# W2's ternary blocks moved to the second turn and off GpSimd; odd relu pieces' upper halves written by ScalarE from PSUM

## The chip, the cores and the metric

The kernel runs on one core of one Trainium2 chip. The metric is the device time of one execution in microseconds (us), lower is better. TensorE, VectorE (DVE), ScalarE (ACT), GpSimd (POOL) and SyncE (SP) each run a queue of instructions of their own; they meet through semaphores. SyncE issues all DMAs.

## The reference

x has 8 sequences of 1024 rows of 512 values. A layer of attention with a compressive memory is followed by a feed-forward layer with ternary weights; each adds to x and ends in a layer norm.

```python
# attention, per segment of 128 rows, 8 heads of 64, carry (mem, z)
q, k, v = x @ Wq, x @ Wk, x @ Wv
sq, sk = elu(q) + 1, elu(k) + 1
att_mem = sq @ mem / (sq @ z)
mem, z = mem + sk.T @ v, z + sk.sum()
att = gate * att_mem + (1 - gate) * (softmax(q @ k.T / 8) @ v)
x = layernorm(x + att @ Wo)
# feed-forward: W -> clip(round(W / (mean|W| + eps)), -1, 1)
h = relu(x @ Wq1.T + b1)            # 2048 wide
x = layernorm(x + h @ Wq2.T + b2)
```

## The kernel before

**Turns.** A turn g (32 of them) takes two sequences' segments of 128 rows, in two halves t. Its steps are spread over three passes of one loop written for each engine, `for g in range(NG + 2)`: in pass g the attention of turn g runs (`project_qk`, `scores`, `project_v`, `turn_p`, `read_memory`, `attend`), the output projection of turn g-1 (`project_out`, then `residual` and `normalise` on VectorE), and the feed-forward of turn g-2 (`ffn_up`, `ffn_down`), whose first `ffn_up` pieces run at the end of pass g-1. The order of all calls in these loops is written out by hand, engine by engine. It, the semaphores and the four PSUM banks 2 to 5 that `take` deals out in rotation set the order of the work.

**fp32 by halves.** Each fp32 operand is an upper and a lower float16 part, and matmuls are done on both. `ffn_up(g, j)` (L430, L431) makes piece j of 8 of the hidden layer, 16 matmuls, in bank 0 or 1. `h_relu` (L1187) on ScalarE writes relu of it as fp32 into one of four buffers `h32`. `h_split` on VectorE converts it to float16 (`h_hi`, L858), and for even j subtracts (L861); for odd j `h_rest` on GpSimd subtracts (L1395). `ffn_down` (L444, L445) takes `h_hi` and `h_lo`.

**Ternary weights.** W1 and W2 are 16 blocks each. For each block two comparisons with a threshold are written as masks into the unused buffer `yt` (L912 below and L913 above on VectorE; for odd blocks the below mask on GpSimd, L1405). `turn_w` (L265, L266) turns and subtracts them in bank 0 or 1 by eight matmuls, and `put_w` (L1215) copies the result to `w1t` or `w2t`. The thresholds come from ScalarE's sums (`w_sum`, L1205) through `threshold` (L895) and `sum_all` (L486). Blocks 0 to 23 are compared in pass 0 and the last ones at its end and in pass 1.

**Copies on the DMA queue.** Transposes of whole tiles between 32x32 blocks are sixteen DMAs each: `move_y` (L1551, waits for both halves' norm), `move_sk` (L1563), `move_att` (L1551). Before and after `move_y` stand `bounce_out` and `bounce_back`: the next turn's maximum of x goes to DRAM and comes back to all partitions as `amax_row`. `update_memory` (L399) on TensorE waits for all sixteen sk copies; VectorE's `all_max` (L615), which stands ahead of `p_split` in its queue, waits for `amax_row`. The waiting lines read:

```python
pe.wait_ge(sem["skblocks"], MOVED * (g + 1))     # update_memory
sp.wait_ge(sem["norm0"], by_t(g, 1))             # move_y
pe.wait_ge(sem["relu"], n - 1)                   # ffn_up, n >= 2
```

## Time and profile before

| what | us |
|---|---|
| median of three runs | 1914.51 (1912.84 to 1919.87) |
| profiled execution, its own time | 1912.87 |
| its span | 1910.9 |
| TensorE busy | 1855.7 |
| VectorE busy | 1449.1 |
| ScalarE busy | 1006.1 |
| GpSimd busy | 794.7 |

The span is from the first to the last recorded instruction; the execution's own time has 2.0 us around it. Busy times add up an engine's instructions, in all stretches, so what a change is worth in one stretch is read from that stretch: from what ends the wait that comes last there.

### The profile page before, as it was taken

Reading aid. Unit: us, or ns where it says so; the run is one execution under the profiler, and the core shown is the slowest. Engines: PE = TensorE matmul, PEld = TensorE weight load, DVE = VectorE, ACT = ScalarE, POOL = GpSimd, SP = SyncE. Lnnn points to the kernel's source line nnn. Section 1 sums busy time; section 2 is a strip of 40 time slices with the busy share of each in tenths; the row PEclk is TensorE's granted clock in tenths of the full one; section 3 lists DMA queues with packets and bytes.
Section 4 is the critical chain, followed back from the end, with each engine's and each line's share of the span. In section 5 each row is a group of like instructions: output and inputs, shape, how many; then the busy total and the mean of one; then the engine's idle time right before and its main releaser. Section 6 shows DMA issues by size and latency. Waiting matters only on the chain.

```text
span 1910.9 us, 44707 instructions
## 1 busy us (share of the span) xinstructions
PE 1855.7 (97%) x16575; PEld 1311.8 (69%) x16575; DVE 1449.1 (76%) x2969; ACT 1006.1 (53%) x2426; POOL 794.7 (42%) x790
## 2 busy tenths in 40 slices
PE   5689999999999999999999999999999999999998
PEld 3566677766777766677766677766677766677765
DVE  7867777777777787777777877777777777777774
ACT  5755555555554555554555554545555645555541
POOL 1813344443344444344444344444345444344443
PEclk9889999999999999999999999999999999999999
DMA  8412333223333233233223333323333322333110
GB/s 270 123 23 46 58 61 66 52 49 59 62 59 65 49 53 61 58 60 65 54 45 64 61 59 64 64 38 60 61 59 63 67 38 59 61 58 62 36 23 23
DMA packets 556422, 117.49 MB, mean 61 GB/s; under 512 B 529824, under 2 KB 533808, under 8 KB 555696
## 3 DMA queue, kind: packets, MB, share of 16 engines
q1 hardware_dynamic: 556208, 114.64, 29.4%
q8 instruction: 134, 2.20, 0.6%
q14 instruction: 80, 0.66, 0.2%
HBM read 50.54 MB, written 16.80 MB: 35 GB/s over the span
## 4 chain that ended last, share of the span: by engine, by line
PE 80%; SPq 7%; DVE 6%; DMA 3%; issue 2%; ACT 1%; POOL 1%; DVEq 0%; POOLq 0%; ACTq 0%
PE bank L431 12%; PE bank L430 12%; PE bank L444 8%; PE bank L445 8%; SPq L1551 7%; PE bank L280 6%; PE bank L282 6%; PE bank L281 6%; PE bank L413 3%; PE bank L411 3%; PE bank L412 3%; PE bank L368 3%; DMA amax_row<-amax_dram 2%; PE bank L294 2%; PE bank L347 2%
## 5 line engine op out<-in xcount | busy, mean ns | idle before, releaser
L430 PE MATMUL bank<-yt,w1t 128*128 128x256 f16 x2048 | 453.9, 273 | 0.0
L431 PE MATMUL bank<-yt,w1t 128*128 128x256 f16 x2048 | 453.9, 273 | 0.0
L1141 ACT ACTIVATE prob<-bank,exp_bias,gscalars 128x128 f32<-128x128 f32 x512 | 227.6, 455 | 356.6 <-DVE exp_bias L723 347.7
L444 PE MATMUL bank<-w2t,arena 128*128 128x512 f16 x1024 | 388.4, 379 | 0.0
L445 PE MATMUL bank<-w2t,arena 128*128 128x512 f16 x1024 | 388.1, 379 | 0.0
L1187 ACT ACTIVATE arena<-bank,b_scaled,wscalars 128x256 f32<-128x256 f32 x512 | 262.9, 569 | 213.4 <-PE bank L431 156.3
L858 DVE CAST arena<-arena 128x512 f16<-128x512 f32 x256 | 154.8, 605 | 89.9 <-ACT arena L1187 89.1
L1317 POOL TENSOR_TENSOR att_mem<-att_mem,gate_in 128x512 f32<-128x512 f32 x60 | 83.1, 1385 | 330.1 <-DVE att_mem L762 318.7
L430 PEld LDWEIGHTS bank<-yt,w1t 128*128 128x128 f16 x2048 | 200.5, 98 | 23.3 <-issue 0.3
L431 PEld LDWEIGHTS bank<-yt,w1t 128*128 128x128 f16 x2048 | 200.3, 98 | 22.7
L1395 POOL TENSOR_TENSOR arena<-arena 128x512 f16<-128x512 f32 x128 | 155.3, 1213 | 87.6 <-DVE arena L858 87.6
L444 PEld LDWEIGHTS bank<-w2t,arena 128*128 128x128 f16 x1024 | 100.1, 98 | 111.9
L445 PEld LDWEIGHTS bank<-w2t,arena 128*128 128x128 f16 x1024 | 100.2, 98 | 110.5
L1353 POOL TENSOR_TENSOR at<-att_dot,at 128x512 f16<-128x512 f32 x60 | 89.7, 1495 | 191.3 <-ACT at L1160 191.3
L673 DVE SCALAR_TENSOR_TENSOR xt<-x_blocks,gscalars,xt 128x512 f16<-128x512 f32 x62 | 83.3, 1343 | 84.7 <-ACT xt L1095 84.7
L280 PE MATMUL bank<-xt,wk_hi 128*128 128x256 f16 x512 | 141.0, 275 | 0.0
L281 PE MATMUL bank<-xt,wk_hi 128*128 128x256 f16 x512 | 140.6, 275 | 0.0
L282 PE MATMUL bank<-xt,wk_lo 128*128 128x256 f16 x512 | 140.6, 275 | 0.0
L280 PE MATMUL bank<-xt,wq_hi 128*128 128x256 f16 x512 | 139.5, 273 | 0.0
L282 PE MATMUL bank<-xt,wq_lo 128*128 128x256 f16 x512 | 139.5, 273 | 0.0
L281 PE MATMUL bank<-xt,wq_hi 128*128 128x256 f16 x512 | 139.5, 273 | 0.0
L718 DVE TENSOR_REDUCE row_max<-bank 128x4 f32<-128x512 f32 x128 | 87.4, 683 | 37.6 <-PE bank L317 37.6
(191 smaller groups left out, 4392.9 us busy)
## 6 DMA issues: line engine op xcount, KB each, us to landing
rows<-in_L_attn_x SPq DMA_DIRECT2D x32, 512.0 KB, 3.6
out_rows<-rows SPq DMA_DIRECT2D x64, 256.0 KB, 2.3
x_blocks<-in_L_attn_x SPq DMA_DIRECT2D x248, 64.0 KB, 2.8
sk<-sk_t SPq DMA_DIRECT2D x480, 32.0 KB, 2.0
att_dot<-att_mem SPq DMA_DIRECT2D x480, 32.0 KB, 2.0
y_blocks<-rows SPq DMA_DIRECT2D x480, 32.0 KB
arena<-in_L_ffn_W SPq DMA_DIRECT2D x6, 1024.0 KB, 5.5
w2t<-in_L_ffn_W SPq DMA_DIRECT2D x2, 1024.0 KB, 13.3
```

The lines of the kernel that those rows point to most:

```text
L280: pe.matmul(ps[:, :, c], w_hi[n][:, k, cols], xt[:, :, k], start=k == 0, stop=False)
L281: pe.matmul(ps[:, :, c], w_hi[n][:, k, cols], xt[:, :, KT + k], start=False, stop=False)
L282: ins = pe.matmul(ps[:, :, c], w_lo[n][:, k, cols], xt[:, :, k], start=False, stop=k == KT - 1)
L430: pe.matmul(ps[:, c], w1t[:, k, cols], yt[:, g % 2, :, k], start=k == 0, stop=False)
L431: ins = pe.matmul(ps[:, c], w1t[:, k, cols], yt[:, g % 2, :, KT + k], start=False, stop=k == KT - 1)
L444: pe.matmul(banks[own][:], h_hi[:, f, toks], w2t[:, f, :], start=f == 0, stop=False)
L445: ins = pe.matmul(banks[own][:], h_lo[:, f, toks], w2t[:, f, :], start=False, stop=f == FT - 1)
L858: dve.tensor_copy(hi, h32[:, n % NH32]).then_inc(sem["h_hi"], 1)
L1141: ins = act.activation(prob[:, t, at], ps[:, c], ACT.Exp, scale=gcol(g, G_EXP), bias=exp_bias[:, t, at:at + 1], accum_out=row_sum[:, t, h: ...
L1187: ins = act.activation(h32[:, n % NH32, c * GT:(c + 1) * GT], ps[:, c], ACT.Relu, scale=w(H_SCALE_Y), bias=b1_scaled[:, f:f + 1])
L1395: pool.tensor_tensor(lo, h32[:, n % NH32], hi, ALU.subtract).then_inc(sem["h_pool"], 1)
L1551: sp.dma_start(to, at).then_inc(done, 16)
```

## The change

- No comparison is on GpSimd any more: VectorE does both of each block, with two pairs of masks instead of four. They lie in one half of `yt`, so that the first turn's `yt` can be written while W2's blocks are still made.
- W1's blocks (0 to 15) stay in pass 0. TensorE turns W2's (16 to 31) in pass 1 and, the last four, at the start of pass 2, in banks 6 and 7. `ffn_up` of turn 0 waits only for W1's blocks; `ffn_down` of turn 0 waits for all 32.
- For odd j, `h_relu` writes `h_hi` from PSUM by a second activation per half piece (L1196 there), and `h_split` is called for even j alone.
- The calls in all engines' loops stand in another order: `update_memory` now closes a pass, after `ffn_up` 0 to 2; on VectorE `normalise` of the first half stands before `group_max`; gates, two loads of W2 and two of x are issued a pass later.

```diff
-        wbelow = yt[:, 0].rearrange("p t k n -> p (t k n)").rearrange("p (b n) -> p b n", b=4)
-        wabove = yt[:, 1].rearrange("p t k n -> p (t k n)").rearrange("p (b n) -> p b n", b=4)
+        masks = yt[:, 1].rearrange("p t k n -> p (t k n)").rearrange("p (m b n) -> p m b n", m=2, b=2)
+        wbelow, wabove = masks[:, 0], masks[:, 1]
...
+        def turned_bank(n):
+
+            return banks[n % 2 if n < NBLOCKS // 2 else 6 + n % 2][:].rearrange("p (j c) -> p j c", j=4)
...
             def turn_w(n):
 
-                ps = banks[n % 2][:].rearrange("p (j c) -> p j c", j=4)
+                ps = turned_bank(n)
                 if n == 0:
                     pe.wait_ge(sem["ident16"], 1)
                 if n >= 2:
                     pe.wait_ge(sem["wput"], n - 1)
-                pe.wait_ge(sem["above"], n + 1)
-                pe.wait_ge(sem["below_pool" if n % 2 else "below"], n // 2 + 1)
+                if n == NBLOCKS // 2:
+                    pe.wait_ge(sem["hscale"], 1)
+                    pe.wait_ge(sem["thr_chain"], 2)
+                pe.wait_ge(sem["masks"], n + 1)
                 for j in range(4):
                     cols = slice(j * P, (j + 1) * P)
-                    pe.matmul(ps[:, j], wabove[:, n % 4, cols], ident16[:], start=True, stop=False)
-                    ins = pe.matmul(ps[:, j], wbelow[:, n % 4, cols], minus16[:], start=False, stop=True)
+                    pe.matmul(ps[:, j], wabove[:, n % 2, cols], ident16[:], start=True, stop=False)
+                    ins = pe.matmul(ps[:, j], wbelow[:, n % 2, cols], minus16[:], start=False, stop=True)
                 ins.then_inc(sem["wturn"], 1)
...
                 else:
-                    pe.wait_ge(sem["wput"], NBLOCKS)
+                    pe.wait_ge(sem["wput"], NBLOCKS // 2)
...
@@ -854,11 +860,12 @@
                 lo = h_lo[:, 2 * j:2 * j + 2].rearrange("p f t -> p (f t)")
                 if g and j == 0:
                     dve.wait_ge(sem["ffn2"], by_t(g - 1, 1))
+                if n == 0:
+                    dve.wait_ge(sem["masks"], NBLOCKS)
                 dve.wait_ge(sem["relu"], n + 1)
                 dve.tensor_copy(hi, h32[:, n % NH32]).then_inc(sem["h_hi"], 1)
-                if j % 2 == 0:
-                    dve.wait_ge(sem["h_hi"], n + 1)
-                    dve.tensor_tensor(lo, h32[:, n % NH32], hi, ALU.subtract).then_inc(sem["h_dve"], 1)
+                dve.wait_ge(sem["h_hi"], n // 2 + 1)
+                dve.tensor_tensor(lo, h32[:, n % NH32], hi, ALU.subtract).then_inc(sem["h_dve"], 1)
...
-                if n >= 4:
-                    dve.wait_ge(sem["wturn"], n - 3)
-                if n % 2 == 0:
-                    dve.tensor_scalar(wbelow[:, n % 4], src, w(BELOW[m]), None, ALU.is_lt).then_inc(sem["below"], 1)
-                dve.tensor_scalar(wabove[:, n % 4], src, w(ABOVE[m]), None, ALU.is_gt).then_inc(sem["above"], 1)
+                if n >= 2:
+                    dve.wait_ge(sem["wturn"], n - 1)
+                dve.tensor_scalar(wbelow[:, n % 2], src, w(BELOW[m]), None, ALU.is_lt)
+                dve.tensor_scalar(wabove[:, n % 2], src, w(ABOVE[m]), None, ALU.is_gt).then_inc(sem["masks"], 1)
...
@@ -1164,7 +1165,7 @@
                     return
                 if g >= 2:
                     act.wait_ge(sem["ffn1"], 8 * (g - 2) + 8)
-                else:
+                elif g == 1:
...
                 ps = banks[n % 2][:].rearrange("p (c t) -> p c t", c=2)
                 if n == 0:
                     act.wait_ge(sem["hscale"], 1)
+                    act.wait_ge(sem["masks"], NBLOCKS // 2 + 4)
                 if n >= NH32:
                     if j % 2:
                         act.wait_ge(sem["h_pool"], (n - NH32) // 2 + 1)
                     else:
                         act.wait_ge(sem["h_dve"], (n - NH32) // 2 + 1)
+                if n == 1:
+                    act.wait_ge(sem["masks"], NBLOCKS)
+                if g and j == 1:
+                    act.wait_ge(sem["ffn2"], by_t(g - 1, 1))
                 act.wait_ge(sem["ffn1"], n + 1)
                 for c in range(2):
                     f = 2 * j + c
                     ins = act.activation(h32[:, n % NH32, c * GT:(c + 1) * GT], ps[:, c], ACT.Relu, scale=w(H_SCALE_Y),
                                          bias=b1_scaled[:, f:f + 1])
+                    if j % 2:
+                        ins = act.activation(h_hi[:, f], ps[:, c], ACT.Relu, scale=w(H_SCALE_Y), bias=b1_scaled[:, f:f + 1])
                 ins.then_inc(sem["relu"], 1)
...
-                pool.wait_ge(sem["h_hi"], n + 1)
+                pool.wait_ge(sem["relu"], n + 1)
                 pool.tensor_tensor(lo, h32[:, n % NH32], hi, ALU.subtract).then_inc(sem["h_pool"], 1)
...
-            def compare(n):
-                m, i, b = block_place(n)
-                src = ffn_raw(m, i)[:, b * 512:(b + 1) * 512]
-                if n in (1, 17):
-                    pool.wait_ge(sem["threshold"], m)
-                pool.wait_ge(*ffn_raw_loaded(m, i))
-                if n >= 4:
-                    pool.wait_ge(sem["wturn"], n - 3)
-                pool.tensor_scalar(wbelow[:, n % 4], src, w(BELOW[m]), None, ALU.is_lt).then_inc(sem["below_pool"], 1)
...
                 if m == 2 and i >= 2:
                     last = 4 * i + 3
-                    sp.wait_ge(sem["above"], last + 1)
-                    sp.wait_ge(sem["below"], last // 2 + 1)
-                    sp.wait_ge(sem["below_pool"], last // 2 + 1)
+                    sp.wait_ge(sem["masks"], last + 1)
...
             for g in range(NG + 2):
                 if g == 1:
+                    gates_back()
+                    load_ffn_w(2, 2)
                     load_ffn_w(2, 3)
                 load_blocks(g + 1)
                 if g == 0:
                     load_ffn_w(2, 0)
+                    gates_out()
                 bounce_out(g + 1)
-                if g == 0:
-                    gates_out()
                 move_y(g - 1)
                 bounce_back(g + 1)
                 if g == 0:
                     load_ffn_w(2, 1)
-                    gates_back()
+                if g == 1:
+                    load_x(1)
                 move_sk(g)
                 move_att(g)
                 put_out(g - 2, 0)
-                if g == 0:
-                    load_x(1)
+                if g == 1:
+                    load_x(2)
                 put_out(g - 2, 1)
-                if g == 0:
-                    load_x(2)
-                    load_ffn_w(2, 2)
```

**TensorE around a middle turn's update of the memory** (v and sk are its operands, yt and w1t those of `ffn_up`, xt and wk_hi those of the k projection). Before:

```order
L430 MATMUL bank<-yt,w1t 128x256
L431 MATMUL bank<-yt,w1t 128x256
L399 MATMUL bank<-v,sk 64x65 [waits s_v1,s_skblocks,s_attd]
L399 MATMUL bank<-v,sk 64x65 x7
L399 MATMUL bank<-v,sk 64x65 [waits s_v1,s_skblocks,s_attm]
L399 MATMUL bank<-v,sk 64x65 x7
L280 MATMUL bank<-xt,wk_hi 128x2x128 [waits s_xt,s_attm]
L281 MATMUL bank<-xt,wk_hi 128x2x128
```

and now:

```order
L436 MATMUL bank<-yt,w1t 128x256
L437 MATMUL bank<-yt,w1t 128x256
L405 MATMUL bank<-v,sk 64x65 [waits s_v1,s_skblocks,s_attd]
L405 MATMUL bank<-v,sk 64x65 x7
L405 MATMUL bank<-v,sk 64x65 [waits s_v1,s_skblocks,s_attm]
L405 MATMUL bank<-v,sk 64x65 x7
L436 MATMUL bank<-yt,w1t 128x256 [waits s_yt,s_relu]
L437 MATMUL bank<-yt,w1t 128x256
```

The update stood behind pieces 3 and 4 of `ffn_up` and ahead of the projection; now it stands behind piece 2 and ahead of piece 3.

**VectorE between the second half's mean and variance and the copies of y, a middle turn** (arena is the piece of the hidden layer, rows the tile that is normalised). Before:

```order
L833 BN_AGGR mean_var<-stats 128x2 [waits s_bn0]
L858 CAST arena<-arena 128x512 [waits s_relu]
L718 TENSOR_REDUCE row_max<-bank 128x4 [waits s_score]
L723 TENSOR_SCALAR exp_bias<-row_max,gscalars 128x4 [waits s_rowmax,s_pexp,s_sc1]
L602 TENSOR_REDUCE amax<-x_blocks 128x1 [waits s_there1,s_xblocks]
L840 TENSOR_SCALAR rows<-rows,mean_var,rstd 128x512 [waits s_rstd0] x2
```

and now:

```order
L839 BN_AGGR mean_var<-stats 128x2 [waits s_bn0]
L724 TENSOR_REDUCE row_max<-bank 128x4 [waits s_score]
L729 TENSOR_SCALAR exp_bias<-row_max,gscalars 128x4 [waits s_rowmax,s_pexp,s_sc1]
L846 TENSOR_SCALAR rows<-rows,mean_var,rstd 128x512 [waits s_rstd0]
L608 TENSOR_REDUCE amax<-x_blocks 128x1 [waits s_there1,s_xblocks]
L846 TENSOR_SCALAR rows<-rows,mean_var,rstd 128x512 [waits s_rstd0]
```

The cast is gone, and the first half is normalised before the maximum of x.

**ScalarE at the end of pass 1** (arena is the relu piece, w2t the place of W2's blocks). Before:

```order
L1095 ACTIVATE xt<-x_blocks,gscalars 128x512 [waits s_qproj,s_kproj,s_xturn,s_vproj,s_xscale]
L1187 ACTIVATE arena<-bank,b_scaled,wscalars 128x256 [waits s_ffn1,s_hscale]
L1187 ACTIVATE arena<-bank,b_scaled,wscalars 128x256
L1187 ACTIVATE arena<-bank,b_scaled,wscalars 128x256 [waits s_ffn1]
L1187 ACTIVATE arena<-bank,b_scaled,wscalars 128x256
L1095 ACTIVATE xt<-x_blocks,gscalars 128x512 [waits s_qproj,s_kproj,s_xturn,s_vproj,s_xscale]
L1187 ACTIVATE arena<-bank,b_scaled,wscalars 128x256 [waits s_ffn1]
```

and now:

```order
L1193 ACTIVATE arena<-bank,b_scaled,wscalars 128x256 [waits s_ffn1,s_masks,s_hscale]
L1193 ACTIVATE arena<-bank,b_scaled,wscalars 128x256
L1193 ACTIVATE arena<-bank,b_scaled,wscalars 128x256 [waits s_ffn1,s_masks]
L1196 ACTIVATE arena<-bank,b_scaled,wscalars 128x256
L1193 ACTIVATE arena<-bank,b_scaled,wscalars 128x256
L1196 ACTIVATE arena<-bank,b_scaled,wscalars 128x256
L1223 ACTIVATE w2t<-bank 128x4x128 [waits s_wturn] x4
L1193 ACTIVATE arena<-bank,b_scaled,wscalars 128x256 [waits s_ffn1]
```

Piece 1 has two activations more and waits for the masks; the copies of blocks 28 to 31 stand behind it and ahead of piece 2.

## Rows read from the trace of the kernel before

**Rows 1.** The page: span, busy time and share of the engines, TensorE in forty slices.
```profile
span 1910.9 us, 44707 instructions
...
PE 1855.7 (97%) x16575; PEld 1311.8 (69%) x16575; DVE 1449.1 (76%) x2969; ACT 1006.1 (53%) x2426; POOL 794.7 (42%) x790
...
PE   5689999999999999999999999999999999999998
```

**Rows 2.** Busy time in stretches, one middle turn: stretch, length, busy by engine (instructions), clock, DMA.
```profile
254.79:311.56 56.77, 56.77 (x515) 40.15 (x516) 44.48 (x93) 30.05 (x74) 24.18 (x24) 1.00 0.30 58
```

**Rows 3.** TensorE's waits in the first 140 us: us in total, times, longest.
```profile
PE bank L265 <- POOL yt L1405: 2.8, 9, 0.6
```

**Rows 4.** Lines of the blocks: ns min/median/max, first and last start, forms.
```profile
L912 DVE TENSOR_SCALAR yt<-w2t,wscalars x4: 473/480/486, 58.5 to 65.2; 128x512 f16<-128x512 f32 x4
...
L913 DVE TENSOR_SCALAR yt<-arena,wscalars x24: 473/820/909, 67.6 to 95.1; 128x512 f16<-128x512 f32 x24
...
L1405 POOL TENSOR_SCALAR yt<-arena,wscalars x12: 1717/1982/2355, 68.1 to 94.1; 128x512 f16<-128x512 f32 x12
...
L1215 ACT ACTIVATE w2t<-bank x16: 591/597/598, 79.9 to 96.8; 128x512 f16<-128x512 f32 x16
```

**Rows 5.** VectorE and TensorE in order of time, first and second turn: start, length, line.
```profile
32.95 2.28 DVE L865 TENSOR_REDUCE wscalars<-arena 128x1 f32<-128x2048 f32 x1
...
99.14 0.27 PE L282 MATMUL bank<-xt,wk_lo 128*128 128x256 f16 x1
...
130.65 0.27 PE L430 MATMUL bank<-yt,w1t 128*128 128x256 f16 x1
```

**Rows 6.** Busy time in stretches around an idle time of TensorE.
```profile
35.00:39.20 4.20, 0.28 (x3) 0.12 (x4) 4.10 (x10) 3.69 (x5) 0.00 (x0) 0.91 0.93 249
39.20:45.00 5.80, 5.80 (x36) 3.11 (x37) 5.15 (x11) 5.71 (x9) 2.08 (x1) 0.50 0.76 219
```

**Rows 7.** The conversion among the page's costliest groups: busy us, mean ns, idle before and its releaser.
```profile
L858 DVE CAST arena<-arena 128x512 f16<-128x512 f32 x256 | 154.8, 605 | 89.9 <-ACT arena L1187 89.1
```

**Rows 8.** ScalarE in order of time, a relu piece of the last turn.
```profile
1882.67 1.02 ACT L1187 ACTIVATE arena<-bank,b_scaled,wscalars 128x256 f32<-128x256 f32 x2 [0.73 <-PE bank L431]
```

**Rows 9.** The DMA queue in order of time: start of the first issue, length of all.
```profile
181.10 11.54 SPq L1563 DMA_DIRECT2D sk<-sk_t  x16
...
294.29 11.21 SPq L1563 DMA_DIRECT2D sk<-sk_t  x16
...
453.22 14.46 SPq L1551 DMA_DIRECT2D y_blocks<-rows  x16
```

**Rows 10.** Line 1563, copies of sk; then updates of the memory, from the chain of waits.
```profile
DMA to landing us min/median/max: 1.9/2.0/5.3
...
139.55 1.08 PE bank L399 x32
...
196.39 1.08 PE bank L399 x32
...
311.56 1.08 PE bank L399 x32
...
1739.01 1.08 PE bank L399 x32
```

**Rows 11.** VectorE, GpSimd and the DMA queue in order of time, before one turn's copies of y.
```profile
335.40 0.39 DVE L858 CAST arena<-arena 128x512 f16<-128x512 f32 x1
...
336.53 1.10 DVE L723 TENSOR_SCALAR exp_bias<-row_max,gscalars 128x4 f32<-128x4 f32 x1
337.55 1.21 DVE L602 TENSOR_REDUCE amax<-x_blocks 128x1 f32<-128x1024 f32 x1
338.68 0.98 DVE L840 TENSOR_SCALAR rows<-rows,mean_var,rstd 128x512 f32<-128x512 f32 x2
...
336.46 1.15 POOL L1395 TENSOR_TENSOR arena<-arena 128x512 f16<-128x512 f32 x1
...
339.69 10.40 SPq L1551 DMA_DIRECT2D y_blocks<-rows  x16
```

361 lines of the change are left out of this document (168 added, 193 removed).

## The prediction

> **What bounds the kernel now.** Read the page first: TensorE is busy for 97% of the span, and its forty slices are full but for the first three [rows 1]. A stretch of one middle turn says the same: 56.77 us long, TensorE busy for all of it, VectorE for 44.5, ScalarE for 30.0, GpSimd for 24.2 [rows 2]. So a cheaper piece on VectorE or ScalarE gives nothing by itself. 55 us of the span are idle on TensorE (1910.9 - 1855.7), some 43 of them in the first 250 us. The rest lies in middle turns: the updates of the memory mark them, and from the first to the last listed are 28 turns [rows 10]: (1739.01 - 139.55) - 28 x 56.77 = 9.9 us over the floor. What can change the time is: the first two turns, these 9.9 us, new waits that the order of work makes, and the last turn. TensorE's matmuls themselves are the same in kind and number.
>
> **First turn (slower start, then faster blocks).** GpSimd set the pace of W1 and W2: 1.98 us for its one comparison of every second block, while VectorE took 0.48 for one alone and 0.82 in the middle beside GpSimd [rows 4]. TensorE's own waits for it are small, 2.8 us [rows 3], since VectorE's queue is held too. Now each block costs VectorE two comparisons in a row: 2 x 0.41 (pipelined; 0.48 each alone), 0.82, and with two pairs of masks this runs on, TensorE's 0.45 to 0.86 being less. Against that, the first comparison (58.5 before [rows 4]) comes later: Wo's maximum, 2.28 us [rows 5], now stands before the second k split, and the second half of Wv's split before the V projection. Following the queues, I put the first comparison at 61.9. The first eight blocks wait for exponentials that share ScalarE's queue, to 69.4; the next eight take 8 x 0.82, to 77. Attend, the memory update and the threshold of W2 follow, then k's first projection, blocks 16 to 19 and k's second projection, which ends at about 89.5, against 99.25 before (the last of its matmuls starts at 99.14 and holds TensorE for 0.11) [rows 5]: **9.7 us earlier**.
>
> **Second turn.** From there to the first matmul of the FFN it was 130.65 - 99.25 = 31.4 us [rows 5]. This is a chain through all engines (projection, residual, scores, exponentials), and blocks 20 to 27 now stand inside it: the comparisons of 20 to 23 between the two residuals, those of 24 to 27 before V's split, 3.3 us on VectorE for each four. About half of the 6.6 is hidden: I take 3.0. The FFN starts at 123.9, a lead of 6.7.
>
> **What is moved beside them.** VectorE's threshold of W2 now waits for TensorE's sum, which stands behind both updates of the memory; behind it in VectorE's queue stand the second attention scaling and blocks 16 to 19. That wait is inside the 89.5. Of the DMA queue, the gates and the last two quarters of W2 and the second and third x go behind the sk copies of the first turn; the gates land at about 72, before GpSimd's first product near 80, and x blocks of the next turn are 90 at the latest, before the maximum at 107: nothing. In middle turns GpSimd's first inverse deviation of the output stands behind the gate products, and with it an output copy; it has till the queue's next free place, 10 us later: nothing.
>
> **Blocks 28 to 31** cost the most of it. Two masks are free, so the comparisons of 30 and 31 wait for TensorE's blocks 28 and 29; ScalarE's relu piece 1 waits for all masks, because it writes where W2 lies; and it stands ahead of the copies that block 30 waits for. TensorE: 4 x 0.45 of work, and an idle time of comparisons 1.3 (part beside block 29) + relu piece 2.05 + a copy 0.6 [rows 4], 3.9 us. Lead left: 6.7 - 1.8 - 3.9 = **1.0 us**. Then the clock: after 4.2 us with 0.28 busy the granted clock was 0.50 (the lower of 1.2 and 2.4 GHz) for the next 5.8 us, which cost 2.9 [rows 6]. I take the same: **+2.9**. Bounds: 0, if the idle time is too short, and twice that.
>
> **Relu pieces.** 128 casts of 0.605 us leave VectorE [rows 7], 77 us, worth nothing in a full TensorE turn. ScalarE gets 256 writes of 128x256; two such took 1.02 us [rows 8], so an odd piece takes 2.05 instead of 1.02, 4.1 us per turn, into 26 us of idle time. Where pieces of the FFN follow each other every 1.74 us [rows 8], the piece after next waits for an odd one: 0.06 + 2.05 + 0.05 - 1.74 = 0.4. In a middle turn the memory update (1.1 us) or a projection stands between. In the last turn nothing does: pieces 3, 5, 7, **+1.3**.
>
> **Middle turns.** The update of the memory now stands before FFN pieces 3 and 4, 3.5 us of matmuls earlier. It waits for sixteen copies of sk, whose queue starts after the sixteen copies of y. In one turn the sk issues ran from 181.10 for 11.54 us [rows 9]; an issue is 0.6 long and lands 1.9 after its start [rows 10], so the last lands at 193.9, while the update would start at 196.39 - 3.5 = 192.9 [rows 10]: 1.0 late. In another they end at 305.5 and land at 306.8, the update would start at 308.1 [rows 9, 10]: no wait. What decides is the length of the y issues, 10.4 [rows 11] to 14.5 us [rows 9]. Done for all 28 turns, with the stalls that they have already, 15 would wait, 21.7 us in sum. But the y queue also starts earlier. Before it, VectorE did a cast (0.39), the score maximum, its bias, x's maximum and two normalisations, and the bias took 1.10 because GpSimd had started its 1.15 us subtraction at 336.46 [rows 11]. Without the cast the bias is done by 336.45, and the second normalisation ends near 338.6 instead of 339.7: 1.0 us. Taking 1.0 from each of the waits, none below zero, leaves 8.3. Against 9.9 now: **-1.6 us**. Bounds: +11.8 with no earlier start, -9.9 with no wait at all.
>
> A rule weighed here. Comparisons 28 and 29 run beside GpSimd's gate products; the row has a median of 0.82 us for such a comparison [rows 4], which ends before the update is through, so it costs nothing. The Trainium skill (SBUF — State Buffer, "SBUF: two separate sides") says that the pair of ports which VectorE and GpSimd share is an exclusive lock, held for a whole instruction, and the loser waits it out. By that rule the two would end up to 1 us after TensorE wants them, and the sum would be 1 us more.
>
> **Sum.** -1.0 + 2.9 + 1.3 - 1.6 = +1.6 us. The profiled execution took 1912.87 us (span 1910.9), the lower end of the three runs; their median is 1914.51. On that median the forecast is **1916 us**. About 0.5% (9.6 us) is what a measurement of this kernel can tell from no change; this is far inside.
>
> **The rivals.**
> *Slower: the sk wait becomes the rule.* One mechanism: the copies of y and sk go through one queue, and the update waits for the last in every turn. The mean of the 15 late turns is 1.45 us without an earlier start; in all 28: 40.5 - 9.9 = +31, and 1914.5 + 31 + 3.2 = 1949. It decides from the point where the last sk copy lands after FFN piece 2 in quick turns too; there it has 1.2 us to spare. Half of it, 1930, needs only that GpSimd's subtraction still delays the bias. For it: the margins are smaller than the spread of the issues. Against: the removed cast.
> *Faster: the lead stays.* If blocks 28 to 31 wait for little and the middle turns' 9.9 go mostly: 1914.5 - 6.7 + 1.8 + 1.3 - 9 = 1902. For it: VectorE has 5 us less in each turn. Against: a relu piece stands ahead of block 30's copy, whatever the speed.
> *The change does nothing in the middle turns* because the waits there are on the queue of copies alone: that is the forecast with 0 for its term, 1917.5.
>
> **How the numbers follow.** The forecast with its bounds (middle turns -9.9 to +11.8, first two turns 3 either way, clock 0 to 5.8) reaches from 1903 to 1927; chance 0.68, of which 0.20 for the third rival, whose time lies within it. Slower by over 0.5% (over 1924): 0.20, faster by over 0.5% (under 1905): 0.12. The range goes a little into the slower rival: 1903 to 1930.
>
> **What would show it.** VectorE's comparisons near 0.48 us with no GpSimd beside them; k's second projection of the second turn ending near 89.5; the FFN's first matmul near 124; TensorE idle 3 to 5 us after the second turn's update, and a granted clock of 0.5 behind it; in some ten middle turns a wait of the update's matmul for sk, about a microsecond each; three gaps of 0.4 in the last turn. Wrong would be: middle turns of 58 us or more throughout (the slower rival), a first FFN matmul before 118, or waits for ScalarE's longer odd pieces in middle turns.

## Result and profile after

The changed kernel took **1932.26 us** (median of four runs, 1928.85 to 1936.42), the kernel before beside it 1913.67 us (1912.15 to 1919.87): ratio 1.0088, 95% interval 1.0071 to 1.0105. It is slower by more than the 0.5% that can be told from no change. The forecast was 1916 us and a range of 1903 to 1930: both too low, and "slower" had had a chance of only 0.20. The profiled execution took 1928.85 us, 16 us more than the one before.

The page of the changed kernel (span, engines with their busy time, share and instructions, TensorE in forty slices, its granted clock), answering to [rows 1]:

```profile
span 1926.9 us, 44818 instructions
...
PE 1857.8 (96%) x16575; PEld 1313.5 (68%) x16575; DVE 1458.9 (76%) x2857; ACT 1122.9 (58%) x2682; POOL 768.3 (40%) x774
...
PE   4779999999999999999999999999999999999998
...
PEclk8799999999999999999999999999999999999999
```

TensorE's busy time is nearly the same as before (the lines of [rows 1]); the span grew by 16, so its idle time grew, from 55.2 to 69.1 us, and some of its busy time ran at the lower clock. VectorE, which lost 128 conversions, is as busy as before; the last section says why.

**Where the 16 us lie.** The updates of the memory are marks again. They now stand 3.49 us of matmuls earlier in the work (two FFN pieces), so 3.49 is added where a time is set beside one of [rows 10]. From the chain of waits (start, length) and the timeline of TensorE (in brackets: idle before, releaser):

```profile
137.98 1.15 PE bank L405 x32
...
203.43 1.15 PE bank L405 x32
...
262.82 1.15 PE bank L405 x32
...
1748.03 1.15 PE bank L405 x32
```

```profile
132.13 0.30 PE L436 MATMUL bank<-yt,w1t 128*128 128x256 f16 x1
```

```profile
143.90 0.29 PE L271 MATMUL bank<-ident,yt 128*128 128x128 f16 x1 [3.77 <-ACT w2t L1223]
```

| stretch | before | after | later by | forecast |
|---|---|---|---|---|
| first FFN matmul | 130.65 | 132.13 | 1.5 | -6.7 |
| from there to the third turn's update, less 3.49 before (196.39 - 3.49 and 203.43) | 62.25 | 71.3 | 9.05 | 1.8 + 3.9 + 2.9 = 8.6 |
| 27 turns to the last update | 1542.6 | 1544.6 | 2.0 | -1.6 |
| from there to the end of the span (after: less 3.49) | 171.9 | 175.4 | 3.5 | 1.3 |

The sum is 16. The forecast had 1.6 in its place. More than half of the 14.4 between them is the first row: 8.2, a lead of 6.7 us that did not come.

**TensorE's waits after 140 us** (total, times, longest), the changed kernel:

```profile
PE bank L405 <- issue: 7.9, 12, 1.1
PE bank L271 <- ACT w2t L1223: 3.8, 1, 3.8
PE bank L436 <- ACT arena L1196: 2.1, 6, 0.4
```

L405 is the update's matmul. It waits for sk in twelve turns, at most 1.10 us, 7.9 in sum. L271 is block 30, held by ScalarE's copy. L436 is an FFN piece, held by the relu piece before the last.

**Behind block 29's idle time the clock is low** (stretch, length, busy by engine, clock):

```profile
139.50:144.00 4.50, 0.73 (x14) 0.56 (x12) 4.14 (x16) 2.57 (x6) 0.57 (x1) 0.83 0.33 51
144.00:149.20 5.20, 5.20 (x33) 4.15 (x33) 1.55 (x5) 2.44 (x5) 0.59 (x1) 0.50 0.36 51
```

In the second stretch TensorE is busy throughout at a granted clock of 0.50, the lower of its two levels.

### The profile page after: what moved, and what is told of

It is laid out like the page before. It is cut to its first block, busy times and chain, and to the rows that moved or that the text cites. A ratio compares the mean times of both kernels' runs of the same rounds, so it can differ in the third digit from the quotient of the medians.

```text
span 1926.9 us, 44818 instructions
## 1 busy us (share of the span) xinstructions
PE 1857.8 (96%) x16575; PEld 1313.5 (68%) x16575; DVE 1458.9 (76%) x2857; ACT 1122.9 (58%) x2682; POOL 768.3 (40%) x774
## 4 chain that ended last, share of the span: by engine, by line
PE 89%; DVE 4%; SPq 2%; DMA 2%; ACT 2%; issue 1%; POOL 0%; POOLq 0%; DVEq 0%; ACTq 0%
PE bank L436 12%; PE bank L437 11%; PE bank L452 11%; PE bank L453 10%; PE bank L286 6%; PE bank L288 6%; PE bank L287 6%; PE bank L374 3%; PE bank L419 3%; PE bank L418 3%; PE bank L417 3%; PE bank L353 3%; PE bank L300 2%; PE bank L302 2%; PE bank L301 2%; SPq L1527 2%
## 5 line engine op out<-in xcount | busy, mean ns | idle before, releaser
L436 PE MATMUL bank<-yt,w1t 128*128 128x256 f16 x2048 | 456.1, 273 | 2.1 <-ACT arena L1196 2.1
L1193 ACT ACTIVATE arena<-bank,b_scaled,wscalars 128x256 f32<-128x256 f32 x512 | 275.0, 564 | 255.1 <-PE bank L437 213.1
L1329 POOL TENSOR_TENSOR att_mem<-att_mem,gate_in 128x512 f32<-128x512 f32 x60 | 89.3, 1488 | 393.3 <-DVE att_mem L768 393.3
L1365 POOL TENSOR_TENSOR at<-att_dot,at 128x512 f16<-128x512 f32 x60 | 78.9, 1315 | 393.7 <-ACT at L1161 393.7
L436 PEld LDWEIGHTS bank<-yt,w1t 128*128 128x128 f16 x2048 | 200.7, 98 | 28.7 <-ACT arena L1196 3.8
L1196 ACT ACTIVATE arena<-bank,b_scaled,wscalars 128x256 f16<-128x256 f32 x256 | 143.8, 562 | 0.0
L868 DVE TENSOR_TENSOR arena<-arena 128x512 f16<-128x512 f32 x128 | 127.0, 992 | 4.4
```

What stands on the lines that cost most here:

```text
L436: pe.matmul(ps[:, c], w1t[:, k, cols], yt[:, g % 2, :, k], start=k == 0, stop=False)
L868: dve.tensor_tensor(lo, h32[:, n % NH32], hi, ALU.subtract).then_inc(sem["h_dve"], 1)
L1193: ins = act.activation(h32[:, n % NH32, c * GT:(c + 1) * GT], ps[:, c], ACT.Relu, scale=w(H_SCALE_Y), bias=b1_scaled[:, f:f + 1])
L1196: ins = act.activation(h_hi[:, f], ps[:, c], ACT.Relu, scale=w(H_SCALE_Y), bias=b1_scaled[:, f:f + 1])
```

## The first turn: who held the lead

In both kernels ScalarE's first copy of a turned block stands behind all eight sums of |W1| and |W2|. The issues of the DMA queue and ScalarE in order of time, the kernel before:

```profile
40.76 0.34 SPq L1520 DMA_DIRECT2D arena<-in_L_ffn_W  x1
43.51 0.34 SPq L1536 DMA_DIRECT2D amax_dram<-amax  x1
...
50.87 0.33 SPq L1543 DMA_DIRECT2D amax_row<-amax_dram  x1
53.75 0.33 SPq L1520 DMA_DIRECT2D arena<-in_L_ffn_W  x1
```

```profile
61.35 2.00 ACT L1205 ACTIVATE rows<-arena 128x2048 bf16<-128x2048 f32 x1
...
63.47 0.60 ACT L1215 ACTIVATE w1t<-bank 128x512 f16<-128x512 f32 x1
```

and the changed kernel:

```profile
45.26 0.34 SPq L1496 DMA_DIRECT2D arena<-in_L_ffn_W  x1
...
46.38 0.33 SPq L1512 DMA_DIRECT2D amax_dram<-amax  x1
56.18 0.32 SPq L1519 DMA_DIRECT2D amax_row<-amax_dram  x1
56.55 1.02 SPq L1496 DMA_DIRECT2D arena<-in_L_ffn_W  x1
```

```profile
65.05 1.91 ACT L1213 ACTIVATE rows<-arena 128x2048 bf16<-128x2048 f32 x1 [2.19 <-DMA arena<-in_L_ffn_W]
...
67.44 1.07 ACT L1223 ACTIVATE w1t<-bank 128x512 f16<-128x512 f32 x2
```

The first load is W2's first quarter, the write of x's maximum (amax_dram) stands behind it, then its reading back, then the load of W2's second quarter. In the changed kernel the first load waits for the second half of Wv's split, which VectorE now does behind the gates and a score maximum: 45.26 instead of 40.76. The maximum then lands only by 56.18, 9.8 us after its issue (7.4 before), and the second quarter's load, which had been free since GpSimd's split of Wo ended at 47.97, goes out at 56.55 instead of 53.75. Its sum starts at 65.05 instead of 61.35, and the first copy comes at **67.44 instead of 63.47**, 4.0 us late, although the first comparison came at 62.12, as forecast (61.9). The working of the forecast had the blocks wait for comparisons and exponentials alone; the sum ahead of the first copy was not in it.

> The changed kernel with two things of its first turn moved: the second half of Wv's split stands on VectorE right behind q's second split (before the gates and the score maxima), and the load of W2's second quarter stands on the DMA queue ahead of the wait for x's maximum. Everything else as changed. Theory A (the lead was lost because ScalarE's first copy of a block waits for the last of the eight sums, whose quarter of W2 was loaded from 56.55 on, behind the wait for x's maximum, and was there at 65.05; and because the V projection started at 45.33 instead of 41.10): the load is issued at about 48, V starts at about 42, blocks 0 to 7 are done at about 70 instead of 74.8, k's second projection of the second turn ends about 91.5 instead of 95.6, the first FFN matmul comes at about 128 instead of 132.13, and the whole takes 1928, 4 us less than 1932.3. Theory B (two pairs of masks and TensorE's lower clock set the pace of the blocks, whoever feeds the sums): block 7 is done no more than 1 us earlier, the FFN starts at 131 or later, 1931 to 1932.

```diff
 (VectorE)
+                if g == 0:
+                    w_split("v", 1)
                 residual(g - 1, 0, 0)
                 if g == 0:
                     gates()
...
                 normalise(g - 1, 0, 0)
-                if g == 0:
-                    w_split("v", 1)
 (SyncE)
+                if g == 0:
+                    load_ffn_w(2, 1)
                 bounce_back(g + 1)
-                if g == 0:
-                    load_ffn_w(2, 1)
```

Measured: 1925.74 us against 1913.73, ratio 1.0059 (1.0036 to 1.0082). The load went out at 49.47, the sum started at 62.95 (behind the exponentials), the first copy at 65.32. Block 7 was done at 72.12, later than the 70 expected, k's second projection at 92.48 (changed: 95.60), the FFN started at 128.69 (132.13). Theory A holds for the lead, 3.4 us of it against the changed kernel's trace (4.1 expected); theory B is not wholly out, since the blocks came at a slower pace than expected.

> The changed kernel with only the load of W2's second quarter moved ahead of the wait for x's maximum on the DMA queue; Wv's split stays where the change put it. Theory A (the last of the eight sums held ScalarE's first copy of a block, and its load stood behind the wait for the maximum): the load is issued at 48 to 49 instead of 56.55 and ScalarE has the sum done before its exponentials of 61, so that blocks 0 to 7 are done by 72 to 73 instead of 74.8, with the V projection still at 45.3; FFN at 129 to 130. Theory B (Wv's split and with it the V projection carry the loss): block 7 is done at 74 or later and the FFN starts at 130.5 or later.

Only the SyncE part of the diff above. One run, 1929.45 us, where the interval of the whole is wider than what is sought; its trace says more. V started at 45.49, the load went out at 48.15, the first copy came at 65.44, as with both moves, and block 7 was done at 72.74. But k's first projection then ran at the low clock in part (4.45 us for 24 matmuls that take 2.78), and the FFN started at 131.40. Expected were 129 to 130 by A, 130.5 or later by B: the moved load gives blocks and not, by itself, the FFN. In the runs below that left the first turn as changed, the last sum started at 63.9 to 65.9 and the FFN at 130.05 to 131.72, since the load's landing differs from run to run; so a gain under 1.5 us at this mark is not shown by one trace, and the 3.4 of the run before are 1.4 to 3.4 against five traces of the changed first turn.

> The run with the last quarter's load and Wv's split moved, with four pairs of masks for the sixteen blocks of W1 (the other half of yt lies free in the first turn) instead of two; W2's sixteen keep two. Theory A (with two pairs each comparison waits for the block before the last, so that blocks run one after the other with gaps of 0.2 to 0.5 us on TensorE; in the kernel before with comparisons on VectorE and four pairs, eight blocks took 5.3 us, here 6.5): blocks 8 to 15 take 5.5 us instead of 6.5, blocks 0 to 7 save another 0.5 to 1, and the FFN of the second turn starts at 127.0 to 127.7 instead of 128.69; 1924 against 1925.7. Theory B (ScalarE's copies and exponentials set the pace, masks don't matter): blocks 8 to 15 in 6.3 us or more, FFN at 128.3 or later.

```diff
+        def pair(n):
+            return (n // 2 % 2 if n < NBLOCKS // 2 else 0), n % 2
...
-                if n >= 2:
-                    dve.wait_ge(sem["wturn"], n - 1)
+                if n >= 4:
+                    dve.wait_ge(sem["wturn"], n - 3 if n < NBLOCKS // 2 else n - 1)
```

Blocks 8 to 15 took 5.7 us (72.15 to 77.87) instead of 6.5 (72.77 to 79.27), and the FFN started at 126.94: 1.75 us sooner, as A expected; the run with four repairs, below, has the same first turn as the run it is set against and started at 128.75, so the 1.75 are more than that spread. **Two pairs of masks cost 1.75 us.** The whole took 1923.99 us, ratio 1.0076 (1.0059 to 1.0093); against the run without it (1.0059, intervals overlapping) the whole doesn't show so little.

## Blocks 28 to 31 and the clock

> The changed kernel with ScalarE's relu piece 1 of the first group waiting for 28 masks instead of 32 (its upper halves lie where the third quarter of W2 lay, the lower halves, where the last quarter lies, are GpSimd's, which waits for all 32 now). Theory A (blocks 30 and 31 waited 3.8 us because the relu piece of 2.05 us waited for all masks and stood ahead of the copies; and TensorE's clock fell behind that idle time, about 2.8 us more): the piece runs beside the FFN's matmuls, the idle time falls from 3.77 to about 1.3 us, the granted clock behind it stays at 1.0, and the whole takes 1927, 5.3 us less than 1932.3. Theory B (the copies or the comparisons set the pace, the relu piece only stands beside them): idle time 3 us or more, 1931 to 1932. If the idle time falls to 1.3 but the clock still falls: 1929.8.

```diff
                 if n == 1:
-                    act.wait_ge(sem["masks"], NBLOCKS)
+                    act.wait_ge(sem["masks"], NBLOCKS - 4)
...
+                if n == 1:
+                    pool.wait_ge(sem["masks"], NBLOCKS)
                 pool.wait_ge(sem["relu"], n + 1)
```

Measured: 1924.72 us, ratio 1.0050 (1.0035 to 1.0065). Block 30's first matmul in TensorE's timeline, and the stretches around it:

```profile
138.21 0.22 PE L271 MATMUL bank<-ident,yt 128*128 128x128 f16 x1 [0.62 <-DVE yt L919]
```

```profile
137.60:138.20 0.60, 0.00 (x0) 0.02 (x1) 0.60 (x3) 0.60 (x2) 0.00 (x0) 1.00 0.34 56
138.20:141.40 3.20, 3.00 (x34) 2.67 (x35) 3.10 (x9) 2.18 (x6) 1.40 (x1) 1.00 0.31 47
```

The idle time is 0.62 us (A expected 1.3) and the clock behind it 1.0. From the FFN's first matmul to the end of piece 3 it took 11.25 us (130.10 to 141.35) instead of 17.07 (132.13 to 149.20): **5.8 us**. The median of the whole fell by 7.5; what that has over 5.8 lies inside the intervals. The comparisons, alone on the path now, hold TensorE for 0.62.

> The changed kernel with 48 matmuls of 128x128 of the identity (their result is read by nobody) into a free bank of TensorE, between blocks 29 and 30, where it stood idle for 3.77 us; nothing else is moved. Theory A (the idle time itself lets TensorE's clock fall: 0.5 behind it, which costs the blocks 30 and 31 about 1.0 us and the FFN's piece 3 about 1.7 us): with the gap filled, the granted clock stays at 1.0, blocks 30 and 31 take 0.9 to 1.1 instead of 1.88 us and piece 3 takes 1.9 instead of 3.6; the stretch from the update to the end of piece 3, 11.2 us in the changed kernel, takes 8.5. Theory B (the clock would have fallen there anyway, or the slow matmuls wait for something else): 10.5 us or more.

```diff
+                if n == 30:
+                    b = 2 + turn[0] % 4
...
+                    for _ in range(48):
+                        pe.matmul(banks[b][:, 0:P], ident16[:], ident16[:], start=True, stop=True)
```

Busy time in stretches with the gap filled:

```profile
137.50:141.30 3.80, 2.72 (x49) 2.54 (x46) 3.66 (x15) 2.46 (x6) 0.45 (x1) 1.00 0.33 51
141.30:144.20 2.90, 2.88 (x34) 2.65 (x35) 0.67 (x3) 2.45 (x5) 0.71 (x1) 1.00 0.33 52
```

Blocks 30 and 31 took 1.11 us (1.88), piece 3 took 1.91 (3.62), and from the update to the end of piece 3 it was 8.8 us instead of 11.2: **2.4 us are the clock's price** alone (forecast 2.9). The order of the real work is the same, and block 30 starts 5.9 us behind the update in both, so it is the idle time that lets the clock fall. The price differs from trace to trace: behind the same 3.8 us of idle time, piece 3 took 3.59 to 3.62 us in three traces, the changed kernel's among them, but 2.56 and 2.58 in two others, where the clock was back at 1.0 about 3 us behind the idle time; there the price is 1.4. The Trainium skill (TensorE: Matmul & The Clock Gate, "HAM oscillation — how this bites in real kernels") says that idle gaps between matmuls bring the lower clock back, and the trace agrees. The whole, 1931.21 in two runs, does not show it: this trace lost more in the middle turns (18.8 us over 27 turns, 11.8 in the changed kernel's).

## The middle turns: two prices tied together

> The changed kernel with the update of the memory one FFN piece (1.75 us of matmuls) later from the third turn on, behind piece 3 instead of piece 2. Theory A (the update waits for the last sk copy, in 12 of 27 middle turns, 0.3 to 1.1 us each, 7.3 us in sum, and nothing else stands behind it): all these waits are gone, since the longest is 1.10, and the whole takes 1925, 7 us less than 1932.3. Theory B (the waits hide others of ScalarE or VectorE, or the queue of copies only moves the loss to the next place): other waits of 3 us or more in sum appear in the middle turns and the whole takes 1929 or more.

```diff
                 ffn_up(g - 2, 3)
+                if g > 2:
+                    update_memory(g - 1, 0)
+                    update_memory(g - 1, 1)
...
                 ffn_up(g - 1, 2)
-                update_memory(g, 0)
-                update_memory(g, 1)
```

Measured: 1932.83 us, ratio 1.0097 (1.0068 to 1.0126): nothing gained. Its waits after 140 us:

```profile
PE bank L436 <- ACT arena L1200: 9.7, 27, 0.4
```

No wait for sk is left, but piece 3 waits for ScalarE in every turn, and most turns take 57.30 instead of 56.77 us. **A microsecond of update between pieces 2 and 3 had hidden the longer relu piece 1.** That is theory B; that the hidden wait would be this one, the expectation had not said.

> The kernel before with the relu part of the change alone: ScalarE writes odd pieces twice, VectorE's four casts a turn are gone; the order of all engines is that of before. Theory A (a piece waits for the relu of the piece before the last; an odd relu piece takes 2.05 us, so piece 3 waits 0.35 to 0.53 us behind pieces 1 and 2 in every turn where nothing stands between them, as in the run with the update one piece later): 28 to 30 waits of 0.35 to 0.5 us, 10 to 14 us in sum, the sk waits stay small: 1921 to 1928 against 1913.7. Theory B (VectorE's 2.6 us a turn are worth more than ScalarE's 4.1 cost): 1913 or less.

```diff
+                    if j % 2:
+                        ins = act.activation(h_hi[:, f], ps[:, c], ACT.Relu, ...)
...
-                h_split(g - 2, 5)
...
-                h_split(g - 2, 7)
...
-                h_split(g - 1, 1)
...
-                h_split(g - 1, 3)
```

TensorE's waits after 140 us:

```profile
PE bank L430 <- ACT arena L1187: 12.2, 34, 0.4
```

1923.06 us, ratio 1.0061 (1.0039 to 1.0083): theory A. Turn after turn is 0.53 to 0.54 over the floor, though each wait shows 0.36 us. The trace explains it: in a row of these matmuls the next one starts after 0.11 us, but each is recorded for 0.27. The first matmul of piece 3 starts 0.63 us behind the last of piece 2 (825.98 and 825.35), so 0.52 us are lost, and 0.16 of them lie under the record of the last matmul. So the relu part alone costs about 10 us in before's order, and the changed order's earlier update pays it with sk waits instead.

> The changed kernel with the relu part undone alone: ScalarE writes an odd piece once, VectorE converts its upper halves as before the change (four casts of 0.4 to 0.6 us a turn back in its queue, behind or beside the even pieces' splits). Theory A (the part costs the gaps between pieces in the last turns, 2.1 us, and otherwise buys about a microsecond for the y copies in every turn): the gaps of 0.34 to 0.36 are gone, but the update's waits for sk grow from 7.3 us to 15 or more, and the whole takes 1936 to 1942. Theory B (VectorE's time is worth nothing, the y copies start when GpSimd's part is ready): the sk waits stay near 7.3 and the whole takes 1930, 2 us less. Theory C (the longer pieces of ScalarE and GpSimd's subtraction beside VectorE's cost more than the trace shows): 1926 or less.

The diff is the one above with its signs turned, in the changed kernel.

1939.14 us, ratio 1.0132 (1.0093 to 1.0170): theory A by its time. The interval touches the changed kernel's (1.0071 to 1.0105), but the trace agrees: its 27 middle turns are 27.0 us over the floor, against 9.2 to 18.8 in six traces of the changed order. By its cause only in part (TensorE's waits from 140 to 1750 us):

```profile
PE bank L405 <- issue: 9.9, 13, 1.6
PE bank L388 <- issue: 4.5, 3, 1.7
PE bank L374 <- DVE pt_lo L738: 3.8, 4, 1.1
```

The waits for sk are 9.9 us, not 15; the rest stands at two other places, the attention's values (L388) and the reading of the memory (L374), which wait for VectorE's queue. In the longest of them VectorE itself had waited for x's maximum, which comes back on the DMA queue behind the copies of y. In the changed order VectorE's time is worth something, against "worth nothing" in the forecast.

> The changed kernel with the first turn's two moves (last quarter's load and Wv's split), the relu piece that waits for 28 masks, and, from the third turn on, k's first projection between FFN pieces 2 and 3 and the update of the memory behind piece 3, so that an odd relu piece has the projection beside it and the sk copies 4.5 us more; VectorE adds to the memory behind its split of piece 2. If the three losses are independent and these the causes: 1932.3 - 6.5 (first turn) - 5.9 (relu piece and clock) - 7.3 (sk waits) = 1912.6, with no waits for ScalarE between pieces in the middle turns. If the wait only moves on (VectorE stands in the update's place, or the projection waits for x): 1917 or more, with new waits of 0.2 us or more in each turn.

```diff
+                if g > 2:
+                    project_qk(g, "k", 0)
                 ffn_up(g - 2, 3)
+                if g > 2:
+                    update_memory(g - 1, 0)
+                    update_memory(g - 1, 1)
...
-                mem_add(g, 0)
                 normalise(g - 2, 1, 1)
-                mem_add(g, 1)
                 h_split(g - 1, 2)
                 scalars(g + 1, 2)
+                mem_add(g, 0)
+                mem_add(g, 1)
```

1910.35 us, ratio 0.9990 (0.9980 to 0.9999). The chain of waits, and TensorE's waits after 140 us:

```profile
198.73 1.08 PE bank L405 x32
...
257.89 1.08 PE bank L405 x32
...
1733.83 1.08 PE bank L405 x32
```

```profile
PE bank L436 <- ACT arena L1203: 2.1, 6, 0.4
```

(1733.83 - 257.89) / 26 = 56.77: twenty-six turns at the floor, none with a wait; the turn ahead of them still loses 2.4 us. The whole gained 1932.3 - 1910.4 = 21.9, expected 19.7, but the near sum hides shares that came out otherwise. Between the two traces, 18.7 us apart, the first turn's moves gave 3.4 us at the FFN's mark (6.5 expected), the relu piece and the clock 5.9 (5.9), the middle turns 9.5 (7.3). So the three repairs add up, and the first was overrated.

> The run with four repairs, with odd pieces of the last three groups written once by ScalarE and converted by VectorE as before. Theory A (the six waits of 0.34 to 0.36 us for ScalarE in the last three turns, 2.1 us in sum, are the whole price of the relu part once k's projection stands behind piece 2): the waits are gone, nothing else appears, 1908.2 against 1910.35. Theory B (VectorE's casts delay the last residuals and the end): 1910 or more.

```diff
-                    if j % 2:
+                    if j % 2 and g < NG - 3:
```

The six waits were gone, and a wait for VectorE of 1.3 us came in their stead at the last output projection, as theory B has it. 1909.35 us, ratio 0.9987 (0.9975 to 0.9998), beside 0.9990 without it: theory A's 2 us is not shown by the whole.

## The comparisons alone, and a faster kernel

> The kernel before with all comparisons on VectorE and none on GpSimd, four pairs of masks and the order of before. Theory A (GpSimd's 1.98 us for every second block set the pace where TensorE waited for it, 2.8 us, and lengthened VectorE's own comparisons): two comparisons take 0.88 in a row, blocks 16 to 31 come sooner, the FFN starts 2 to 4 us earlier than 130.65, and the whole takes 1910 to 1912. Theory B (VectorE's queue gets 6.5 us longer in the first turn and its later work, the scaling of the attention and x's split, comes later): FFN start at 131 or later, 1914 to 1917.

```diff
-                if n % 2 == 0:
-                    dve.tensor_scalar(wbelow[:, n % 4], src, w(BELOW[m]), None, ALU.is_lt).then_inc(sem["below"], 1)
+                dve.tensor_scalar(wbelow[:, n % 4], src, w(BELOW[m]), None, ALU.is_lt).then_inc(sem["below"], 1)
```

1909.65 us, ratio 0.9984 (0.9975 to 0.9994): theory A. The FFN started at 127.54. **Comparisons on VectorE alone are a gain of about 3 us**, and the 2.8 us of TensorE's waits for GpSimd [rows 3] is near it in size. What the change lost in the first turns came with its order and its two pairs of masks, not with this.

> The kernel before with comparisons on VectorE alone, the relu part, and from the third turn on k's first projection between FFN pieces 2 and 3 (x's second split on ScalarE ahead of relu piece 0 for it); the update stays behind piece 4. Theory A (the loss of the relu part in before's order was only the wait of piece 3 for relu piece 1, 0.53 us a turn, and the middle turns of before lost about 10 us to waits of which VectorE's casts were a cause): the first turns are those of the run with comparisons on VectorE (FFN at 127.5, update at 136.4), the middle turns stand at 56.77, and the whole takes 1900 to 1904. Theory B (the projection now waits for x's split, or the copies of sk keep the middle turns late as before): 1908 or more, with a wait in every turn ahead of the projection.

```diff
                 ffn_up(g - 2, 2)
+                if g > 2:
+                    project_qk(g, "k", 0)
                 ffn_up(g - 2, 3)
...
+                if g >= 2:
+                    xt_hi(g + 1, 1)
                 h_relu(g - 1, 0)
                 h_relu(g - 1, 1)
```

(Onto the kernel with the relu part's and the comparisons' diffs.) 1903.27 us, ratio **0.9955 (0.9940 to 0.9970)**, faster than the kernel before by 9 us, and than the changed one by 29. The chain of waits, and TensorE's waits after 140 us:

```profile
136.73 1.08 PE bank L399 x32
...
196.12 1.08 PE bank L399 x32
...
252.88 1.08 PE bank L399 x32
...
1728.81 1.08 PE bank L399 x32
```

```profile
PE bank L430 <- ACT arena L1189: 2.1, 6, 0.4
```

From 196.12 to 1728.81 are 27 turns of 56.77; in the kernel before they were 9.8 us longer [rows 2, 10]. The relu part alone lost 10 us in this order; with k's projection where piece 3 would wait, and the comparisons off GpSimd, it stands in a kernel 6.4 us faster than with the comparisons alone: between the two traces the 27 middle turns give 10.1 us, and the last turns, with the six waits for ScalarE, take 3.3 back. How much of the 6.4 is the relu part's, and how much the projection's place would give without it, was not tried.

## Why the forecast was wrong, step by step

- **First turn, "9.7 us earlier", and "The FFN starts at 123.9, a lead of 6.7": failed.** k's second projection ended at 95.60, not 89.5, and the FFN started at 132.13, 8.2 us behind the forecast. The step that failed is "The first eight blocks wait for exponentials that share ScalarE's queue, to 69.4": they waited for the last of the eight sums, behind a load behind x's maximum. Block 7 was done at 74.79: 5.4 of the 8.2. Mended, with Wv's split, it gave 1.4 to 3.4 at the FFN's mark.
- **The next eight blocks, "8 x 0.82, to 77": right by a slip.** 69.4 + 6.6 is 76, not 77; the 7.6 us that 77 stands for are what was measured (74.79 to 82.39). TensorE was still at the low clock in part (stretches below), and with two pairs of masks a comparison waits for the block before the last; four pairs give 1.75. From there to the projection 0.7 more was lost. The gates, "at about 72", were right: issued at 70.44 and 71.08.
- **Second turn, "About half of the 6.6 is hidden: I take 3.0": too low.** From the projection to the FFN it took 36.5 us instead of 34.4, so 5.1 over the 31.4 of before. All nine other traces with this order have 35.7 to 36.7. TensorE's clock was at 0.50 near the end of the stretch in both kernels (126 to 131 us, before 124 to 130), so that is not the difference; what of it is the blocks' and what the order's was not tried. Some 3 to 5 of the 8.2 us stay without a run of their own, part of these 2.1 among them.

  TensorE in stretches, changed kernel (length, busy, clock, DMA):

```profile
70.00:75.00 5.00, 3.96 (x34) 0.50 0.47 118
75.00:80.00 5.00, 4.17 (x44) 0.74 0.16 34
80.00:85.00 5.00, 4.36 (x104) 1.00 0.84 320
```

  At the lower level a block takes 0.85 us of TensorE, at the higher 0.45.
- **Blocks 28 to 31, "3.9 us" idle and "+2.9": right**, 3.77 and 2.4. In mechanism too. From block 29's end at 140.13 the comparisons ran 1.30 us, relu piece 1 then 1.81 (2.05 forecast), the first copy 0.66. With the relu piece off the path, only 0.62 of the comparisons was left.
- **Relu pieces, "+1.3" in the last turn: mechanism right, size off.** Six waits, not three, in the last three turns: the last two groups have no update that could stand between pieces 2 and 3. They show 0.34 to 0.36 us each, 2.1 in sum; by the starts of the matmuls they cost 3.1, most of the table's last row (3.5).
- **"77 us, worth nothing": wrong in the changed order**, where putting the casts back costs 7 us. And 77 were not saved: taking the casts off made VectorE 51 us less busy in before's order and 56 in the changed one.
- **Middle turns, "-1.6 us": off by 3.6.** The waits for sk, 8.3 forecast, were 7.9, in twelve turns (some ten forecast). What is missing stands in the first turn of the stretch, 2.6 over the floor with only 0.32 of it for sk, and in turns with other waits. Between runs of the same order this stretch varied from 9.2 to 18.8 us over the floor; its last microseconds can't be forecast.
- **The slower rival**, the sk wait in every turn, did not come: sixteen of 27 turns stood within 0.2 us of the floor. That half of it, 1930, is near the measured time is luck: the loss came by another way. **The third rival** had 0 for the middle turns; the 2.0 measured are nearer to it than to -1.6, though the update did wait, as forecast.
- **Port-lock rule, +1 us at comparisons 28 and 29: the hold came, its price did not.** GpSimd's gate product and VectorE's second comparison for block 28, in order of time:

```profile
135.43 1.44 POOL L1337 TENSOR_TENSOR att_mem<-att_dot,gate_out 128x512 f32<-128x512 f32 x1 [2.22 <-DVE att_dot L780]
```

```profile
135.66 1.49 DVE L919 TENSOR_SCALAR yt<-arena,wscalars 128x512 f16<-128x512 f32 x1
```

  The comparison took 1.49 us, not 0.48 or 0.82, and 1.49 or 1.50 at this place in all nine other traces of this order. It cost nothing: the masks of block 29 were ready at 137.94, and TensorE was busy with the update until 139.06. The forecast's 0.82 was measured beside GpSimd's comparisons (TENSOR_SCALAR), not beside its products (TENSOR_TENSOR).
- **What also failed is the range.** Its bounds took 3 us either way for two turns in which five queues were reordered, and the miss there was 8. And 1903 to 1927 does not follow from the bounds that it names: added up, they reach from 1902 (all low) to 1935 (all high), and 1932.26 lies inside. Why less was taken, the forecast does not say.

## What to carry to other kernels

When an order is rewritten, follow every producer of the first consumer through all the queues, the DMA queue among them: here the first copy waited for a sum, a load, and a maximum's way to memory and back. A longer instruction on an engine with spare time (here ScalarE's 2.05 us against 1.75 of a piece) was free only where other work stood between its producer and the one that needs it; look for a step, here the projection, that can be put there. Try the parts one by one: here the comparisons alone gained 3 us, the relu part lost 10 or stood in a gain by what lay between two pieces, and the new order lost what both gave.

## What was not expected of the hardware

VectorE lost 128 casts and was as busy as before, 1459 us against 1449. The new order did that, not the removal. In before's order the same removal took it from 1449 to 1398; in the changed order, from 1515 with the casts put back to 1459 without. In the new order VectorE's instructions begin more often while one of GpSimd's runs. The subtraction that stayed and a tiny operation on 4 columns, in the changed kernel:

```profile
L868 DVE TENSOR_TENSOR arena<-arena 128x512 f16<-128x512 f32 x128 | 127.0, 992 | 4.4
```

```profile
40.81 0.18 DVE L947 RECIPROCAL gate_cols<-gate_cols 128x4 f32<-128x4 f32 x1
41.02 1.93 DVE L949 TENSOR_SCALAR gate_cols<-gate_cols 128x4 f32<-128x4 f32 x1
```

```profile
40.80 2.13 POOL L1385 TENSOR_TENSOR wo_lo<-arena,wo_hi 128x1024 f16<-128x1024 f32 x1
```

The mean of the subtraction (L868) is 0.99 us in the changed kernel, 0.71 in the one before. It has two lengths: 87 of the 128 took 0.69 us, and 41 took 1.52 to 1.68. All 41 began while a TENSOR_TENSOR of GpSimd ran and ended 0.55 us behind its end; none of the 87 did. In the kernel before 2 of 128 were held in this way, with the casts back in the changed order 36, and without them in before's order 3: it goes with the order.

L949, on 128x4, started at 41.02 and ended at 42.95; GpSimd's subtraction of Wo ran from 40.80 to 42.93. So 1.76 us of it are the other's instruction. The reciprocal ahead of it (L947) ran beside the same subtraction in 0.18, and in the kernel before the same operation was not held beside GpSimd's scaling of Wo:

```profile
44.30 0.17 DVE L943 TENSOR_SCALAR gate_cols<-gate_cols 128x4 f32<-128x4 f32 x1
```

```profile
42.92 2.87 POOL L1371 TENSOR_SCALAR arena<-arena,wscalars 128x1024 f32<-128x1024 f32 x1 [40.22 <-ACT wo_hi L1194]
```

The Trainium skill (SBUF — State Buffer, "SBUF: two separate sides") has VectorE and GpSimd lock each other out of a shared pair of ports for a whole instruction, and for VectorE names its two-port modes and operations with two inputs in SBUF. The 41 held subtractions, which have two inputs in SBUF, agree. L949 and the comparison for block 28 were held as long, though the rows don't show whether they ran in a two-port mode; the reciprocal doesn't speak against it. The last row isn't explained by it here. The comparisons of the kernel before are of the same kind: beside GpSimd's own comparisons of 1.98 us they took 0.91 at most [rows 4]. In these rows GpSimd's TENSOR_TENSOR held such an instruction of VectorE to its end, and its TENSOR_SCALAR did not. Whether the holds also made the copies of sk late was not tried apart.

The clock's fall after 3.8 us of idle time cost 1.4 to 2.4 us. It fell behind 2.9 us too, in the run with the casts back (piece 3 took 3.41 us). Idle times of 0.62 us here, and of 1.10 us behind filler matmuls, cost nothing.
